# Storing the turned rows of ten tiles in the first shared pass and loading them again in the last one

## What is computed

```python
x = x + ga * attention(layernorm(x) * (1 + ca) + sa)
h = layernorm(x) * (1 + cb) + sb                 # 2048 rows of 512
scores = softmax(h @ gate_weight.T)              # 8 experts, the best two of each row
g = silu(h @ w_gate.T) * (h @ w_up.T)            # width 352, per expert
y = sum over the row's two experts of weight * (g @ w_down.T)
y = y + swiglu(h, sw_gate, sw_up, sw_down)       # shared expert, width 2 * 352, all rows
x = x + gb * y
```

## Time and profile before

| | us |
|---|---|
| median of 3 runs (1567.68 to 1570.82) | 1568.44 |
| the profiled execution's own time | 1572.1 |
| its span, first to last instruction | 1569.9 |
| PE busy, of that span | 1520.4 |
| DVE busy | 1006.4 |
| ACT busy | 731.9 |
| POOL busy | 713.6 |
| 16 DMA engines: 304.03 MB, mean | 194 GB/s |

### The profile page before, as it was taken

One profiled execution on the slowest core, in us unless ns is written; L12 is line 12 of the kernel. 1 busy time (PEld: TensorE's weight loads), 2 busy tenths in 40 slices (PEclk: granted clock), 3 DMA queues, 4 the chain that ended last, 5 costly groups with the idle time before them and its releaser, 6 DMA issues.

```text
span 1569.9 us, 29503 instructions
## 1 busy us (share of the span) xinstructions
PE 1520.4 (97%) x8844; PEld 1355.2 (86%) x8844; DVE 1006.4 (64%) x2224; ACT 731.9 (47%) x1738; POOL 713.6 (45%) x761
## 2 busy tenths in 40 slices
PE   6899999998999999999999999998999999999998
PEld 3677778887999999999999999988989899999986
DVE  5876676667777777777777777795467322222268
ACT  2542222345666666666666666653331233333333
POOL 2103333346656566656565666667813211111055
PEclk9999999999999999999999999999999999999999
DMA  7334555568757666666757484653333456756455
GB/s 259 134 121 171 199 189 196 204 238 295 236 166 239 188 202 185 213 198 190 214 165 238 147 246 143 224 208 135 123 124 141 168 195 213 285 200 236 147 181 188
DMA packets 203292, 304.03 MB, mean 194 GB/s; under 512 B 80384, under 2 KB 142208, under 8 KB 196048
## 3 DMA queue, kind: packets, MB, share of 16 engines
q1 hardware_dynamic: 196096, 281.80, 53.1%
q0 software_dynamic: 5680, 18.62, 3.9%
q10 hardware_dynamic: 1440, 2.62, 0.5%
HBM read 187.35 MB, written 115.64 MB: 193 GB/s over the span
## 4 chain that ended last, share of the span: by engine, by line
PE 86%; DVE 6%; ACT 2%; issue 2%; DMA 2%; POOL 2%; another core or an unknown queue 0%; POOLq 0%; SPq 0%; ACTq 0%; DVEq 0%
PE bank L1553 45%; PE bank L1648 17%; PE bank L1763 8%; PE bank L1715 7%; PE bank L1746 4%; PE bank L1813 2%; PE bank L1566 1%; PE bank L1849 1%; DMA xin<-ffn_rows 1%; POOL h L1226 1%; ACT prob L1373 1%; DVE h_lo L2027 0%; POOL acc L1218 0%; ACT h_raw L1248 0%; DVE row_max L2200 0%
## 5 line engine op out<-in xcount | busy, mean ns | idle before, releaser
L1553 PE MATMUL bank<-w,xt_hi 128*128 (+2 forms) x1136 | 286.7, 334 | 10.8 <-DVE xt_lo L2176 7.8
L1553 PEld LDWEIGHTS bank<-w,xt_hi 128*128 128x128 f32 x1136 | 200.8, 192 | 17.8 <-issue 8.5
L1553 PE MATMUL bank<-w,xt_lo 128*128 (+2 forms) x568 | 186.1, 328 | 0.0
L1385 ACT ACTIVATE prob<-prob,row_inv 128x128 f32<-128x128 f32 (+3 forms) x256 | 137.2, 560 | 81.9 <-DVE row_inv L2213 81.9
L2349 DVE TENSOR_TENSOR ht_lo<-bank,ht_hi 128x128 fp32r<-128x128 f32 (+1 forms) x213 | 48.4, 282 | 185.0 <-ACT ht_hi L1493 181.2
L1373 ACT ACTIVATE prob<-bank,neg_max 128x128 f32<-128x128 f32 (+3 forms) x256 | 133.6, 525 | 44.0 <-DVE neg_max L2205 44.0
L1553 PE MATMUL bank<-wv_hi,h_hi 128*128 128x256 f32 x512 | 147.0, 287 | 0.0
L1553 PE MATMUL bank<-w,ht_hi 128*128 (+3 forms) x426 | 139.2, 408 | 6.5 <-DVE ht_lo L2349 5.7
L1553 PE MATMUL bank<-wv_hi,h_lo 128*128 128x256 f32 x512 | 144.7, 283 | 0.0
L1553 PE MATMUL bank<-wv_lo,h_hi 128*128 128x256 f32 x512 | 144.7, 283 | 0.0
L2200 DVE TENSOR_REDUCE row_max<-bank 128x1 f32<-128x128 f32 (+3 forms) x256 | 119.8, 489 | 6.6
(11 more groups left out here) (245 smaller groups left out, 4151.6 us busy)
## 6 DMA issues: line engine op xcount, KB each, us to landing
keys<-k_ring SPq DMA_DIRECT2D x64, 512.0 KB, 3.0
ch_raw<-wexp SPq DMA_DIRECT2D x128, 170.0 KB, 3.1
experts_hi<-ch_hi SPq DMA_DIRECT2D x128, 170.0 KB, 2.6
experts_lo<-ch_lo SPq DMA_DIRECT2D x128, 170.0 KB, 2.7
w<-experts_hi SPq DMA_DIRECT2D x10, 2176.0 KB, 7.9
w<-experts_lo SPq DMA_DIRECT2D x10, 2176.0 KB, 14.6
q_transposed<-q_out SPq DMA_DIRECT2D x64, 256.0 KB, 2.0
k_even<-keys SPq DMA_DIRECT2D x16, 1024.0 KB, 5.8
```

The source lines that it names most:

```text
L1385: ins = act.activation(part, part, ACT.Copy, scale=row_inv[:, h, r:r + 1])
L1553: ins = pe.matmul(dst, a, m, start=(k == 0), stop=(k == last))
```

## The change

ACT stores `xt_hi` and `xt_lo` of jobs 6 to 15 to a new array in memory, 256 KB each, right after its `xt_hi` of the next job. Since the slot of job n is written again for job n+2, ACT waits before that write until the store has landed (semaphore `xt_st`). In the last pass nothing is turned or split: SP loads both parts straight into the slots, and PE's gate waits for these loads. The loads stand in SP's order ahead of the stores of `out`. ACT's ten loads of `xin` go. Apart from that, a semaphore is made free: the statistics of the second norm on DVE (`c_stats`) now wait one by one through `link`, which waits for the instruction just issued, where before one wait followed all four.

```diff
+        xt_d = dram("turned_rows", (NB2, 2, P, D))
-        c_stat = sem("c_stat")
+        xt_st = sem("xt_stored")
...
+            sp.wait_ge(xt_st, 32 * NB2)
+            def load_xt(m):
+                sp.wait_ge(up_full, m - 1)
+                for which, part in enumerate((xt_hi, xt_lo)):
+                    sp.dma_start(part[:, m % 2].bitcast(F32).rearrange("p c n -> p (c n)"), xt_d[m - Z0, which])\
+                      .then_inc(xin_ld[m % 2], 16)
+            def store_out(i):
+                sp.wait_ge(*finished(i))
+                sp.dma_start(out_t[:, GATHER[i], :], acc[:, GATHER[i], :]).then_inc(out_st, 16)
+            load_xt(Z0)
             routed(NSLOT - 1, 0)
+            load_xt(Z0 + 1)
             store_y(NSLOT - 1, 0)
-            for i, t in enumerate(GATHER):
-                sp.wait_ge(*finished(i))
-                sp.dma_start(out_t[:, t, :], acc[:, t, :]).then_inc(out_st, 16)
+            load_xt(Z0 + 2)
+            for k in range(2, NB2 - 1):
+                if Z0 + k + 1 < NJ:
+                    load_xt(Z0 + k + 1)
+                store_out(2 * k - 4)
+                store_out(2 * k - 3)
...
-            def load_xin(m, s, tile):
-                act.dma_start(xin[:, s, :].unsqueeze(1), rows_t[:, bass.ds(tile, 1), :]).then_inc(xin_ld[s], 16)
+            def store_xt(n, s):
+                for which, part in enumerate((xt_hi, xt_lo)):
+                    act.dma_start(xt_d[n - NB1, which], part[:, s].bitcast(F32).rearrange("p c n -> p (c n)"))\
+                       .then_inc(xt_st, 16)
...
             def xt_part(n, s):
                 act.wait_ge(xt_full, n + 1)
+                if isinstance(n, int) and NB1 + 2 <= n < NT + 2:
+                    act.wait_ge(xt_st, 32 * (n - 1 - NB1))
...
                     xt_part(n + 1, 1 - s)
-                if tile is not None:
-                    load_xin(n + 3, 1 - s, tile)
+                if isinstance(n, int) and NB1 <= n < NT:
+                    store_xt(n, s)
...
+            def turned(n, s):
+                if isinstance(n, int) and n >= Z0:
+                    return xin_ld[s], R0 * 8 + (n - Z0) // 2 * 32 + 32
+                return xt_ok, n + 1
...
-                    pe.wait_ge(xt_ok, n + 1)
+                    pe.wait_ge(*turned(n, s))
...
-                dve.bn_stats(stat[:, t, :], acc[:, b * TT + t, :]).then_inc(c_stat, 1)
+                link(dve.bn_stats(stat[:, t, :], acc[:, b * TT + t, :]))
             def c_moments(b):
-                dve.wait_ge(c_stat, b * TT + TT)
```

More of the change, by code:

```diff
@@ L927, in _ @@
                     routed(j * 2 + k, k)
+            sp.wait_ge(xt_st, 32 * NB2)
[8 more added lines that the diff above has]
+            load_xt(Z0)
             routed(NSLOT - 1, 0)
+            load_xt(Z0 + 1)
             store_y(NSLOT - 1, 0)
-            for i, t in enumerate(GATHER):
-                sp.wait_ge(*finished(i))
-                sp.dma_start(out_t[:, t, :], acc[:, t, :]).then_inc(out_st, 16)
+            load_xt(Z0 + 2)
[4 more added lines that the diff above has]
+                store_out(2 * k - 3)
+            for i in range(2 * NB2 - 6, NT):
+                store_out(i)
             sp.wait_ge(out_st, 16 * NT)
@@ L1469, in _, with job @@
             walk_steps(act, step)
-            def job(n, s, prev, nxt, tile=None, route=False):
+            def job(n, s, prev, nxt, route=False):
                 act.wait_ge(gt_full, n + 1)
@@ L1535, in _ @@
             for n in range(Z0 - 3, Z0):
-                job(n, n % 2, "routed", True, NB1 + n + 3 - Z0)
+                job(n, n % 2, "routed", n + 1 < Z0)
             for n in range(Z0, NJ):
                 k = n - Z0
-                job(n, n % 2, "routed" if k == 0 else "shared", n + 1 < NJ, NB1 + k + 3 if n + 3 < NJ else None)
+                job(n, n % 2, "routed" if k == 0 else "shared", False)
                 if k >= 2:
@@ L1819, in loaded @@
                     return xg_ld[s], (m - R0 - s) * 8 + 16
-                if isinstance(m, int) and m >= Z0:
-                    return xin_ld[s], R0 * 8 + (m - Z0) // 2 * 16 + 16
                 return xin_ld[s], (m - s) * 8 + 16
             walk_steps(pe, step)
+            def turned(n, s):
+                if isinstance(n, int) and n >= Z0:
+                    return xin_ld[s], R0 * 8 + (n - Z0) // 2 * 32 + 32
+                return xt_ok, n + 1
             def half(n, s, wofs, which, route):
                 if which == 0:
-                    pe.wait_ge(xt_ok, n + 1)
+                    pe.wait_ge(*turned(n, s))
                 if not (isinstance(n, int) and n == 0):
@@ L1949, in _ @@
                 job(n, r % 2, at[r], at[r - 1] if r else W1, free=(y_gb, n - 2) if r < 3 else (y_ev, r - 2),
-                    gathered=r + 1 < NSLOT, ahead=lambda: next_offset(r + 1))
+                    nxt=r + 1 < NSLOT, gathered=r + 1 < NSLOT, ahead=lambda: next_offset(r + 1))
             pe.wait_ge(w_ld[0], 32 * (E // 2 + 1))
-            job(Z0, 1, 0, at[NSLOT - 1], free=(y_ev, NSLOT - 2))
+            job(Z0, 1, 0, at[NSLOT - 1], nxt=False, free=(y_ev, NSLOT - 2))
             for n in range(Z0 + 1, NJ):
                 k = n - Z0
-                job(n, n % 2, 0, 0, nxt=n + 1 < NJ, free=(y_ev, NSLOT + k - 2) if k < 3 else (y_gb, R0 + k - 2))
+                job(n, n % 2, 0, 0, nxt=False, free=(y_ev, NSLOT + k - 2) if k < 3 else (y_gb, R0 + k - 2))
             turn_mid(NJ - 1, (NJ - 1) % 2)
@@ L2590, in _ @@
                     job(j * 2 + k, k, "routed", True)
-            job(Z0 - 1, 0, "routed", True)
+            job(Z0 - 1, 0, "routed", False)
             def combine(i):
@@ L2625, in _ @@
                 k = n - Z0
-                job(n, n % 2, "routed", True)
+                job(n, n % 2, "routed", False)
                 if k >= 2:
```

## The result

| | before | changed |
|---|---|---|
| median, us | 1570.82 (1567.68 to 1574.15, 5 runs) | 1583.92 (1581.67 to 1586.77, 5 runs) |
| ratio, 95% interval | | 1.0087 (1.0064 to 1.0109) |
| profiled execution, us | 1572.1 | 1586.77 |
| its span, us | 1569.9 | 1584.6 |
| mean granted clock | 0.989 | 0.985 |

The changed kernel is slower by 0.87%, 13.7 us of 1570.8 (the two medians are 13.1 apart). The forecast was 1574.3 with a range of 1563.5 to 1578.0: the sign was right, the size was not. Of the distance, 2.4 us are the base: the sum stood on 1568.44, and with two more runs the kernel before has 1570.82. From its base the sum added 5.9 us; the chip added 13.7 by the ratio.

A forecast was written before the change was run, and what follows sets the result against it. PE was taken to bound the routed slots and most of the first shared pass, POOL the last pass. 1568.44 + 8.1 (stores) + 0.4 (statistics) - 2.0 (last pass) = 1574.9, stated as 1574.3 us; range 1563.5 to 1578.

The forecast's parts named there:

- the sum: Whole kernel: median 1568.44 plus 8.1 for stores, plus 0.4 for statistics, less 2.0 in the last pass, 1574.9 us.
- The loads in the last pass: Last pass: loads behind output stores take 7.2 us a job, just under POOL's 7.44, so they hide.
- The formula: Last pass: two jobs take at least 10.4 us plus the time from finished tile to both parts landed.
- loads late: Rival, last pass: loads exceed POOL's period, costing 4.6 us; 1571.4 with free stores, 1579 with late ones; chance 0.11.
- the forecast: Main case, first shared pass: stores land with the weights; chance 0.5, own range 1570.5 to 1577.5 us.
- The stores in the first pass: First shared pass: job 10's stores land with the weights, delaying `xt_hi` of job 12; cost 8.1 us, bounds 0 and about 10.
- The last pass's gain: Last pass: second POOL addition comes 7.5 us sooner than in the profiled execution, 2.0 sooner than without its hold-up.
- the hold-up at job Z0+2: Last pass's third job: DVE's `h_mid` starts 3.23 us late in the profiled execution; the median's executions were trusted to lack it.
- The turns ahead of the first gather: Before the last pass: two turns of 0.44 us go, so POOL's gathers start 0.9 us earlier.
- the prediction's two gains: Last pass: 7.5 us against the profiled execution, 2.0 us against one without the hold-up.
- The statistics: Job 1: three new DVE waits of 0.12 us cost 0.4 us; the others, at most 1.6, cost nothing.

The follow-up runs named there:

- e2: Changed kernel with each pair of last-pass loads issued one job earlier: 1577.62 us, ratio 1.0041 to the kernel before.
- e6: Kernel before plus the stores, their wait and the new statistics, with the old last pass: 1580.88 us, ratio 1.0068.
- e7: Changed kernel with the statistics' own semaphore put back: 1581.94 us, ratio 1.0088 to the kernel before.
- e1: Changed kernel with the second shared weights issued seven row loads earlier: 1573.28 us, ratio 1.0014 to the kernel before.
- e9: Changed kernel with weights issued earlier, last-pass loads one job earlier and the old statistics semaphore back: 1564.85 us, ratio 0.9974 to the kernel before.
- e15: The kernel of e9 run again in another set of runs: 1565.81 us, ratio 0.9985 to the kernel before.
- e3: Changed kernel with both the weights issued seven row loads earlier and the last-pass loads one job earlier: 1569.12 us, ratio 0.9991 to the kernel before.
- e4: Kernel before with only the statistics changed, each waited for by itself: 1571.33 us, ratio 1.0015.
- e10: Changed kernel storing only `xt_hi`, loaded in place of `xt_lo` too, so results lack the low part: 1576.21 us, ratio 1.0047 to the kernel before.
- e13: The kernel of e8 with the last job's `ht_part` ahead of the last gathered tile's combination: 1568.63 us, ratio 1.0020 to the kernel before.
- e16: The kernel of e11 run again, beside e15: 1566.65 us, ratio 0.9986 to the kernel before.
- e5: Kernel before with only the second shared weights issued earlier: 1565.74 us, ratio 0.9998.
- e8: Kernel before with POOL's gathers of the third and fourth tile waiting for the last pass's third up projection: 1569.79 us, ratio 1.0005.
- e11: The kernel of e9 with the last job's `ht_part` ahead of the last gathered tile's combination: 1566.06 us, ratio 1.0000 to the kernel before.
- e14: Kernel before, unchanged, profiled a second time: 1569.09 us, ratio 1.0009.

## Why the prediction was wrong

**The loads in the last pass: this step failed.** It put L, from a finished tile to both parts landed, at 4.0, got 7.2 us a job, and called them hidden "with nothing to spare", so that they added nothing to the sum. L measured 6.7, 6.6 and 6.8. The estimate took one transfer of 3.2 and something for the rest; it left out that SP issues two output stores (0.8 to 1.6 us) and the `hi` load (0.4 to 0.9) ahead of the `lo` load, which then needs 4.0 to 5.2 by itself. The formula was sound: (10.4 + 6.6) / 2 = 8.5 us a job, and the additions came 8.3 to 8.9 apart. So the rival "loads late" came true together with the forecast, which the text priced at 1579; with the base 2.4 higher that is 1581.4. Its price was 4.6 where 3.5 to 7.2 were measured. e2 takes this cost out and gives +6.5, close to the +5.9 of the sum; that is luck in part, since the stores, the statistics and the unforeseen step below cost more than was summed, and the gain in the last pass was larger, too. A cost hidden "with nothing to spare" on an estimate should not have had a chance of 0.11.

**The stores in the first pass: right in the place and the wait, a little small.** 8.1 predicted, steps of 9.2, 9.1 and 9.4 measured (changed, e6, e7), in the changed kernel 7.25 of them idle time and about 2 at the lower clock. The `lo` store landed at 1149.3, 0.7 behind the weights, where "1132.42 + 13.0 plus 1.1" would have given 1148.3 from the weights' new start at 1134.18. The `hi` store landed at 1145.2, 3.5 before the weights, so not every store waits for their end. e1 settles the cause.

By the Trainium skill (DMA: Bandwidth & Descriptors, Queues, rings and completion order), a DMA engine drains a packet of some 9 to 17 descriptors from one queue before it turns to the next. The trace agrees that the two queues share the engines, but not with that grain. Counted by the us in which they start, in the changed kernel's trace, ACT's records of 2,048 B and SP's of 17,408 B run about as often as each other from 1138.7 to 1147:

```
us        17,408 B of SP   2,048 B of ACT   (records; 0.65 and 0.08 us each)
1136      28               0
1137      20               0
1138      24               10
1139      24               20
1140      16               17
1141      22               43
1142      26               20
1143      17               17
1144      29               15
1145      18               16
1146      15               16
1147      0                12
1148      0                70
```

Equal counts alone would also come of whole packets in turn, since a store and a weight transfer have 128 such records each. The starts tell the two apart: ACT's come in groups of 14 to 16, one for each DMA engine, within 0.4 us, and up to 1144 the groups start 0.72 to 0.81 us apart, about the time of one record of either kind (0.65 + 0.08); only at 1141 is a group twice as large. With whole packets, an engine's 8 records of the `hi` store would run in a row, in 0.7 us; they were spread over 5 us. So each 2 KB record waits for one of 17 KB: sharing goes by records, and small ones beside large ones get a small part of the bytes.

**The last pass's gain: its condition was wrong, and 2.0 a little small for the median.** I took the hold-up at job Z0+2 for a property of one execution. `h_mid` waits over 1.3 us there in 10 of the 17 profiles and 0.6 to 0.7 in the rest, and its size varies (11.7, 8.5 and 6.7 between two gates of an unchanged order). In the changed kernel DVE's `h_mid` is late there as well:

```profile
1515.81 0.52 DVE L2396 TENSOR_TENSOR h_mid<-gate_s,bank 128x352 f32<-128x352 f32 x1 [3.65 <-remote]
```

but PE, which needs no split there, goes on, and the two gate copies are 6.9 apart. So, with loads two jobs ahead, the change takes away what the hold-up costs where it is large, 3.9 us of the last pass (75.4 less 71.5), and next to nothing where it is small or missing (71.9 and 71.4 less 71.5). By the medians, e9 and e15, which have neither of the two costs nor the new statistics, are 4.1 and 2.4 us below the kernel before, where the sum took off 2.0. The turns ahead of the first gather gave the 0.9 us that were counted: the changed kernel is 11.4 behind at job 60, and 10.5 at that gather (1505.70 - 0.73 - 1494.46). The rest of the prediction's two gains, 6.6 of the 7.5 and 1.1 of the 2.0, was meant for the stretch, and both were too much. The part behind POOL's last addition gives some back: 20.8 us in the first profile of the kernel before, 22.0 in e3, 22.9 in e9.

**The statistics: small, as said, but in more places.** 0.4 was predicted at job 1, with the others free. The profiles show 0.5 and 0.35 at jobs 4 and 8, about 0.9 beside whatever of job 1's 0.4 reaches the end; the times allow 0 to 2.4.

**Not foreseen:** a step of 1 to 2 us between jobs 13 and 30. It is in the changed kernel and in e1, e2, e4, e7, e10 and e13; it is 0.6 to 0.7 in e6 and e16, under 0.3 either way in e5, e8, e9, e11, e14 and e15, and e3 has one of 1.3 the other way. e13 has neither stores nor new statistics, so the change isn't needed for it; what sets it stays open, and so does its part in the 13.7.

## What to carry to other kernels

A load that is issued behind a finished result costs its own landing plus everything that the same queue issues between the two; count these in order, and if the slack is a few tenths of a us, give the load one more job of lead. Before small stores go out on a second queue, look for what large transfer is in flight on the first: their small records take turns with its large ones, and a wait for them two jobs later inherits much of its length. Where one profile has a wait that nothing in it explains, take a second profile of the same kernel before building a term on it.

## What the runs showed of the hardware

- A 256 KB store of 2 KB records that lands in 2.0 us on free queues took 14.1 us next to 4.3 MB of 17 KB records (the pair's first took 10.4). ACT's queue moved nothing for 3.9 to 4.0 us from the first issue there, in all five profiles with stores behind the weights (changed, e2, e6, e7, e10); for the other nine pairs of the changed kernel it was 0.8 to 2.4.
- Two profiles of one kernel differed by 3.2 us in one place with no change at all (11.7 and 8.5 between two gate copies; 6.7 in e5, which has the same orders there). DVE's `h_mid` is late there, by up to 3.65 us over all kernels, for a release that the trace can't name. Its cause stays open. Whether the signal or the work of PE itself is late can't be read, since ends of matmuls are modelled.
- PE ran at 1.2 GHz (granted clock 0.50) for the 4 us behind 7.25 us without work, and its twelve matmuls after 4.8 us without took 3.94 where 1.94 is usual.
- A wait of DVE for the instruction it has just issued put the starts 0.72 apart in place of 0.60, for the same two operations.
